# An attention and FFN kernel: transposed rows stored by GpSimd, transposes moved, and FFN seams interleaved with scores and V

## The reference

```python
# layer 1, for each of 8 batches; q = layernorm(x), k = v = cx
t = Wt @ v;  p = Wp @ q;  g = Wg @ k              # 512x512 by 512x2048
att = sum over each of 8 channel groups of p * g  # one number for a group
y = blockdiag(Wz) @ (att * t)                     # 8 blocks of 64x64
x = x + groupnorm(y) * gn_w + gn_b + v
# layer 2, for each row of layernorm(x), columns permuted, 16 heads of 128
h = gelu(t_head @ up[head])                       # 128 -> 512
out = h @ down[head]                              # 512 -> 128
x = x + unpermuted(out)
```

## Time and profile before

| | us |
|---|---|
| median of 3 runs | 1728.28 (1726.62 to 1729.94) |
| the profiled execution | 1731.32 |
| its span in the trace | 1729.5 |
| TensorE busy (matmuls) | 1550.4 (90%) |
| VectorE busy | 1306.9 (76%) |
| ScalarE busy | 919.1 (53%) |
| GpSimd busy | 718.4 (42%) |
| DMA, mean over the span | 218 GB/s |

### The profile page before, as it was taken

How to read it: one execution, slowest core, us unless ns; L and a number is a source line. 1 busy time by engine, 2 the same in 40 slices (tenths; PEclk the granted TensorE clock), 3 DMA queues, 4 the chain that set the end, 5 groups by cost and what they waited for, 6 DMA issues and landing times.

```text
span 1729.5 us, 19276 instructions
## 1 busy us (share of the span) xinstructions
PE 1550.4 (90%) x6592; PEld 1239.7 (72%) x6592; DVE 1306.9 (76%) x1872; ACT 919.1 (53%) x949; POOL 718.4 (42%) x589
## 2 busy tenths in 40 slices
PE   7898668789998899989999899998999889997998
PEld 6676556668776787767877677776877668765886
DVE  5767957877797868867698676987869786886665
ACT  4333425633576337843478234783357723676786
POOL 1333106301682117800287013960159301676785
PEclk9999989999999999999999999999999999999999
DMA  9988865785477835777266781769627693359675
GB/s 367 371 289 323 239 190 175 258 275 180 135 248 230 275 91 196 242 204 238 100 219 219 209 266 61 246 204 280 208 103 238 208 293 127 122 142 271 220 249 207
DMA packets 184512, 376.87 MB, mean 218 GB/s; under 512 B 24544, under 2 KB 98272, under 8 KB 176096
## 3 DMA queue, kind: packets, MB, share of 16 engines
q1 hardware_dynamic: 163936, 308.52, 55.5%
q0 software_dynamic: 20480, 67.13, 11.8%
HBM read 289.55 MB, written 86.03 MB: 217 GB/s over the span
## 4 chain that ended last, share of the span: by engine, by line
PE 42%; DVE 16%; DMA 9%; ACT 7%; issue 6%; SPq 4%; POOL 2%; POOLq 0%; DVEq 0%; ACTq 0%
PE PP L785 15%; PE PP L824 11%; PE PP L839 10%; PE PP L798 4%; DMA xg_scratch<-FB 4%; DVE Z L1051 3%; DMA RAW<-in_cT 3%; SPq L1249 3%; DVE FB L1083 3%; DVE R L1093 2%; PE PP L771 2%; ACT R L906 2%; DVE HX L1093 2%; DVE R L943 1%; DMA WW<-w_scratch 1%
## 5 line engine op out<-in xcount | busy, mean ns | idle before, releaser
L771 PE MATMUL PP<-R 128*128 128x512 f32 x1536 | 370.6, 398 | 65.4 <-DVE R L943 63.1
L824 PE MATMUL PP<-G,WW 128*128 128x512 f32 x1536 | 396.2, 395 | 17.9 <-DMA WW<-w_scratch 10.1
L785 PE MATMUL PP<-R,WC 128*128 128x512 f32 x1536 | 359.3, 396 | 37.1 <-ACT Z L876 28.5
L771 PEld LDWEIGHTS PP<-R 128*128 128x128 f32 x1536 | 289.0, 191 | 144.3 <-ACT R L864 44.5
L785 PEld LDWEIGHTS PP<-R,WC 128*128 128x128 f32 x1536 | 293.8, 192 | 101.8 <-ACT Z L876 30.3
L824 PEld LDWEIGHTS PP<-G,WW 128*128 128x128 f32 x1536 | 290.3, 191 | 88.6 <-issue 24.7
L839 PE MATMUL PP<-R,WW 128*128 128x512 f32 x1050 | 274.9, 398 | 43.8 <-DVE R L1093 32.7
L906 ACT ACTIVATE R<-PP 128x1024 fp32r<-128x1024 f32 x175 | 179.9, 1028 | 193.9 <-PE PP L824 193.0
L839 PEld LDWEIGHTS PP<-R,WW 128*128 128x128 f32 x1050 | 195.8, 190 | 96.3 <-issue 52.3
L907 ACT ACTIVATE PP<-PP 128x1024 f32<-128x1024 f32 x256 | 261.8, 1023 | 0.0
L864 ACT CAST R<-RAW 128x1024 fp32r<-128x1024 f32 x128 | 129.4, 1044 | 244.4 <-DMA RAW<-in_cT 225.7
(11 more groups left out here) (74 smaller groups left out, 1602.5 us busy)
## 6 DMA issues: line engine op xcount, KB each, us to landing
WW<-w_scratch SPq DMA_DIRECT2D x152, 512.0 KB, 5.2
RAW<-in_xT SPq DMA_DIRECT2D x64, 512.0 KB, 7.0
RAW<-in_cT SPq DMA_DIRECT2D x64, 512.0 KB, 8.1
X<-in_x SPq DMA_DIRECT2D x32, 1024.0 KB, 6.9
RAW<-in_cx SPq DMA_DIRECT2D x32, 1024.0 KB, 8.0
xg_scratch<-FB SPq DMA_DIRECT2D x112, 256.0 KB, 4.4
w_scratch<-WW SPq DMA_DIRECT2D x16, 1024.0 KB, 8.7
HX<-wp_scratch SPq DMA_DIRECT2D x8, 1024.0 KB, 9.1
```

What stands on the lines that cost most here:

```text
L771: t = eng.matmul(s_bank(c1), l[:, part(c1)], r, start=(dt == 0 and j == 0), stop=(dt == ND - 1 and j == 2))
L785: t = eng.matmul(PP[2 + ot // 2][:, ot % 2, :], WC[:, l, ct, part(ot)], u[:, r + ct, :], start=(ct == 0 and j == 0), stop=(ct == NT - 1 an ...
L824: t = eng.matmul(PP[slot["up", f, p]][:, e, :], wt[:, l, part(2 * p + e)], g[:, r, :], start=(j == 0), stop=(j == 2))
```

## The change

- `store_x` moves from SP to GpSimd, with the same wait for its block of transposes and the same four DMAs. The buffers and semaphores are the same.
- The four transpose blocks (and the stores, one step behind each) get due times from the table TURN, counted from the next batch's base: for batch 1 from 3.8, 6.8, 9.8, 12.8 to 4, 8, 12, 17.4; for batches 2 to 6 from 1.4, 4.4, 7.4, 10.4 to 3, 5.6, 9.6, 17.4. Batches 0 and 7 keep theirs.
- End of the FFN: `s_mm` becomes one stage for each column block. From batch 2 on the blocks of the first four steps are due by column: c1 = 0 of steps 0 to 3 from -1 to -0.4, then the last but one down step (0), c1 = 1 of the four steps (0.5 to 1.1), the last down step (1.5), and then c1 = 2 and 3. The splits of the first four steps move 1.8 steps ahead, those of steps 4 to 7 get times of their own (S_LATE), the first two loads move 2 steps ahead. The banks of up are counted from the end of the FFN, so that the last three use PP0, PP2, PP3 in this order and PP0 is free.
- Start of the FFN: the first up step goes to f0 - 1, ahead of V's last block (-0.5), the second to f0. `g_hi` and `g_lo` of the first unit move 0.7 ahead, `g_var_b` goes from f0 + 2.7 to f0 + 3.9, `x1_piece` from f0 + 4.8 to f0 + 5, `add_r` from td + 0.56 to td + 0.45.

```diff
--- before.py
+++ after.py
@@ -24,8 +24,12 @@
 EPS = 1e-5
 NRAW = 3
 NFB = 6
+TURN = [(17.9, 21.1, 24.3, 27.5), (4, 8, 12, 17.4)] + [(3, 5.6, 9.6, 17.4)] * 5
 SBT = 5
-UPS = (2, 3, 0)
+UPS = (0, 2, 3)
+S_EARLY = ([(-1 + 0.2 * dt, 0.5 + 0.2 * dt) for dt in range(4)],
+           [(2.0, 2.5), (2.25, 2.75), (3.0, 3.25), (3.5, 3.75)])
+S_LATE = {4: 2.55, 5: 2.8, 6: 3.3, 7: 4.4}
 
 
 def units(i):
@@ -121,14 +125,13 @@
         give(n.up("slo", i, dt), ("raw", slot["s", i, dt // 2]))
         order.append(("s_lo", i, dt))
 
-    def s_mm(i, dt):
+    def s_mm(i, dt, c1):
         if dt == 0:
-            for c1 in range(NT):
-                free["sb", i, c1] = take(("PP", c1 // 2, c1 % 2))
-        for c1 in range(NT):
-            t = n.up("smm", i, dt, c1)
-        give(t, s_half(i, dt))
-        order.append(("s_mm", i, dt))
+            free["sb", i, c1] = take(("PP", c1 // 2, c1 % 2))
+        t = n.up("smm", i, dt, c1)
+        if c1 == NT - 1:
+            give(t, s_half(i, dt))
+        order.append(("s_mm", i, dt, c1))
 
     def load_x(i, ct):
         free["x", i, ct] = take(("X", ct))
@@ -347,19 +350,16 @@
     def turn(i, q, ct):
         if ct == 0:
             if i < B - 1:
-                slot["tb", i, q] = None
-                free["tb", i, q] = take(*[("FB", k) for k in range(4)])
+                slot["tb", i, q] = [("FB", k) for k in range(4)]
             else:
-                k = slot["tb", i, q] = ring("raw", NRAW)
-                free["tb", i, q] = take(("raw", k))
+                slot["tb", i, q] = [("raw", ring("raw", NRAW))]
+            free["tb", i, q] = take(*slot["tb", i, q])
         t = n.up("tr", i, q, ct)
         give(t, ("Z", q, ct))
         order.append(("turn", i, q, ct))
 
     def store_x(i, q):
-        t = n.dma("xg", i, q, sem=f"xg{q}", count=4)
-        k = slot["tb", i, q]
-        give(t, *([("FB", k) for k in range(4)] if k is None else [("raw", k)]))
+        give(n.dma("xg", i, q, sem=f"xg{q}", count=4), *slot["tb", i, q])
         order.append(("store_x", i, q))
 
 
@@ -413,9 +413,9 @@
         give(n.up("radd", f), ("SM", b % 2))
         order.append(("resid", f, b))
 
-    def up_mm(f, p, kk, w):
-        slot["up", f, p] = UPS[kk % 3]
-        free["up", f, p] = take(*banks(UPS[kk % 3]))
+    def up_mm(f, p, k, w):
+        slot["up", f, p] = k
+        free["up", f, p] = take(*banks(k))
         t = n.up("up", f, p)
         give(t, ("WW", w % 2, 0))
         if p:
@@ -531,11 +531,13 @@
         y0, v0, f0 = s0 + 16, s0 + 32, s0 + 36
         first = i == 0
         for j in range(8):
-            put(s0 + 0.3 if (i, j) == (1, 2) else s0 + 2 * j - (5 if j or i else 10), load_s, i, j)
+            put(s0 + 0.3 if (i, j) == (1, 2) else s0 + 2 * j - (10 if i == j == 0 else 7 if i > 1 and j < 2 else 5), load_s, i, j)
         for dt in range(ND):
-            put(s0 + dt - 2.6, s_hi, i, dt)
-            put(s0 + dt - 2.4, s_lo, i, dt)
-            put(s0 + dt, s_mm, i, dt)
+            t = s0 + (dt - 2.6 if i < 2 else dt - 4.4 if dt < 4 else S_LATE.get(dt, dt - 2.6))
+            put(t, s_hi, i, dt)
+            put(t + 0.2, s_lo, i, dt)
+            for c1 in range(NT):
+                put(s0 + (dt + 0.25 * c1 if i < 2 or dt > 3 else S_EARLY[c1 // 2][dt][c1 % 2]), s_mm, i, dt, c1)
         for q in range(NQ):
             for ct in range(NT):
                 t = s0 + 8.4 + 2.6 * ct + 0.3 * q if i == 1 else s0 + (4 * q + ct) * 0.85 + (3.9 if first else 0.9)
@@ -573,21 +575,21 @@
         put(y0 + 1, load_wph, i)
         put(y0 + 12.1, load_wpl, i)
         for ot in range(NT):
-            put(v0 + ot, v_mm, i, ot)
-            put(v0 + ot + 0.95, v_att, i, ot)
+            put(v0 + ot + (0.5 if i and ot == NT - 1 else 0), v_mm, i, ot)
+            put(v0 + ot + (1.4 if i and ot == NT - 1 else 0.95), v_att, i, ot)
         put(v0 + 3.4, aggr_y, i)
         put(f0 + 1.2, g_mean_mm, i)
         put(f0 + 1.25, g_mean, i)
         put(f0 + 2.3, g_var_mm, i)
         put(f0 + 2.35, g_var_a, i)
         put(f0 + 2.4, g_root, i)
-        put(f0 + 2.7, g_var_b, i)
+        put(f0 + 3.9, g_var_b, i)
 
 
         last = i == B - 1
         sp = 2.6 if i < 2 else 4 if last else 6
         for ct in range(NT):
-            x0 = f0 + 4.8 + sp * ct
+            x0 = f0 + 5 + sp * ct
             for hf in range(2):
                 put(x0 + hf * sp / 6, x1_piece, i, ct, hf)
             for q in range(NQ):
@@ -603,7 +605,7 @@
         for ct in range(NT):
             put(e + 1 + 0.5 * ct if i == 0 else e + 1.6 + 0.8 * ct, xln2, i, ct)
         for q in range(NQ):
-            t = f0 + 17.9 + 3.2 * q if i == 0 else e + 4.6 + (2 if last else 3) * q
+            t = base[i + 1] + TURN[i][q] if not last else e + 4.6 + 2 * q
             for ct in range(NT):
                 put(t + 0.25 * ct, turn, i, q, ct)
             put(t + 1, store_x, i, q)
@@ -614,21 +616,23 @@
         end = len(gs)
         for g, (b, h, x) in enumerate(gs):
             lead = f0 + 2 * g
-            put(max(lead - 6, v0 - 2), gather, f, b, h)
-            put(lead - 2.3, g_hi, f, b)
-            put(lead - 2.1, g_lo, f, b)
+            put(max(lead - 6, v0 - 3 if g == 0 else v0 - 1), gather, f, b, h)
+            put(lead - (2.3 if g else 3.0), g_hi, f, b)
+            put(lead - (2.1 if g else 2.8), g_lo, f, b)
             put(lead - 1.5, resid, f, b)
             for p in range(2):
                 kk = 2 * g + p
-                tu = f0 + (kk - 1 if kk > 1 else 0.5 * kk)
-                td = f0 + (kk + 1.5 if kk < 2 * end - 2 else kk + 1 if kk < 2 * end - 1 else kk + 0.5)
-                td = min(td, f0 + 2 * end - (1 if kk == 2 * end - 2 else 0.5))
-                put(tu, up_mm, f, p, kk, w + x)
+                left = 2 * end - kk
+                tu = f0 + (kk - 1 if kk else -1)
+                td = f0 + kk + 1.5
+                if left < 3:
+                    td = f0 + 2 * end + (-0.5 * left if last else (1.5, 0)[left - 1])
+                put(tu, up_mm, f, p, UPS[(kk - 2 * end) % 3], w + x)
                 put(tu + 0.6, gelu, f, p, kk, i)
                 put(tu + 1.2, h_lo, f, p)
                 put(td, dn_mm, f, p, w + x)
                 w_used[w + x] = (tu + 0.55, td + 0.55)
-            put(min(td + 0.56, f0 + 2 * end - 0.01), add_r, f)
+            put(td + 0.45, add_r, f)
             put(td + 0.6, scatter, f, b, h)
             f += 1
         for x, (h, bs) in enumerate(ws):
@@ -738,8 +742,8 @@
         return PP[3][:, 1, :] if i == 0 else PP[1][:, 1, :]
 
     def tb_tile(i, q):
-        k = slot["tb", i, q]
-        t = FB[:, 0:4, :] if k is None else RAW[k][:]
+        name, k = slot["tb", i, q][0]
+        t = FB[:, 0:4, :] if name == "FB" else RAW[k][:]
         return t.rearrange("p a n -> p (a n)").rearrange("p (b c r) -> p b c r", b=16, c=4)
 
     def perm_of(h):
@@ -758,19 +762,18 @@
                     if ct % 2:
                         t.then_inc(S["wc"], 1)
             elif stage == "s_mm":
-                i, dt = a
+                i, dt, c1 = a
                 pe.wait_ge(*at["shi", i, dt])
                 pe.wait_ge(*at["slo", i, dt])
                 xh, ch = s_tile(i, dt, 0)[:, 0, :], s_tile(i, dt, 0)[:, 1, :]
                 xl, cl = s_tile(i, dt, 1)[:, 0, :], s_tile(i, dt, 1)[:, 1, :]
-                for c1 in range(NT):
-                    if dt == 0:
-                        for t in free["sb", i, c1]:
-                            pe.wait_ge(*t)
-                    for j, (l, r) in enumerate(((xl, ch), (xh, cl), (xh, ch))):
-                        t = eng.matmul(s_bank(c1), l[:, part(c1)], r, start=(dt == 0 and j == 0),
-                                       stop=(dt == ND - 1 and j == 2))
-                    t.then_inc(S["smm"], 1)
+                if dt == 0:
+                    for t in free["sb", i, c1]:
+                        pe.wait_ge(*t)
+                for j, (l, r) in enumerate(((xl, ch), (xh, cl), (xh, ch))):
+                    t = eng.matmul(s_bank(c1), l[:, part(c1)], r, start=(dt == 0 and j == 0),
+                                   stop=(dt == ND - 1 and j == 2))
+                t.then_inc(S["smm"], 1)
             elif stage == "y_mm":
                 i, q, ot = a
                 for t in free["y", i, q, ot]:
@@ -1148,6 +1151,13 @@
                 pool.wait_ge(*at["perm",])
                 eng.indirect_dma_start(out=FB[:, f % NFB, :], out_offset=None, in_=xg_d[b][:, :],
                                        in_offset=perm_of(h)).then_inc(S[f"fb{f % NFB}"], 16)
+            elif stage == "store_x":
+                i, q = a
+                pool.wait_ge(*at["tr", i, q, NT - 1])
+                for r in range(4):
+                    eng.dma_start(
+                        xg_d[i][cols(q), part(r)].rearrange("(b j) c -> j b c", j=32),
+                        tb_tile(i, q)[32 * r:32 * r + 32].rearrange("j b c r -> j b (c r)")).then_inc(S[f"xg{q}"], 16)
             elif stage == "resid":
                 f, b = a
```

(7 more changed lines are left out.)

## The result

| | before | after |
|---|---|---|
| median of runs in alternation (range), us | 1729.11 (1726.24 to 1735.05) | 1733.45 (1731.82 to 1736.72) |
| profiled execution, us | 1731.32 | 1731.82 |
| its span, us | 1729.5 | 1730.0 |

The ratio of the times is 1.0033, with a 95% interval of 1.0018 to 1.0048. The change makes the kernel 0.33% slower, 4 us by the medians and 6 by the ratio, where the prediction had 52 us faster. The time lies outside the range.

A forecast was written before the change was run, and what follows sets the result against it. TensorE was taken as the bound, its idle time as the price. Terms -24 (scores), -8 (batch 1's Y), -6 (FFN end), -18 (FFN start), +4 (last FFN) sum to -52 us: 1676 us from median 1728.28, range 1652 to 1722.

The forecast's parts named there:

- What bounds: Whole kernel: TensorE, busy 90% of the span, is the bound; a change is worth the TensorE idle time it removes.
- A block costs 5.6 us and lands 9.5 us after the transposes: Scores: GpSimd issues four stores at 1.4 us each; the block lands 3.9 us after its last issue, 3.5 steps after transposes.
- Block 0 ends at step 4, block 1 can then start at 7.5: Scores, batches 2 to 7: block 1, due at 5.6, costs 0.5 us; stage losses fall from 62 to 38, gain 24 us.
- The wait that I expected to cost 40 us or more: Sign to look for: the wait of VectorE's transposes for stores to land stays at 40 us or more.
- The fourth block in the Y stage: Last transpose block moved to step 17.4, in the next batch's Y stage; forecast difference there 0 us.
- Batch 1's Y stage: Without the store on SP the sums' broadcast goes out some 9 us earlier; gain 8 us, 15 us hole under 7.
- The end seam: FFN end into scores: early score blocks give the last down step 9.5 us; 1 of 3.4 us gained at six seams, 6 us.
- The start seam: FFN start: group variance behind the subtraction lets the fourth down step start earlier; 2.6 us at seven seams, 18 us gained.
- The last FFN stage: Sixteen stores at 1.4 us need 22.4 us of GpSimd's 14.5 us room; time lost, +4 us.
- (A): Rival: GpSimd's issue is slow, 2.5 us or more, and becomes the bound; total about 1762 us, slower; chance 14%.
- (B): Rival: DMA engines bound the scores, 48.8 us a stage; gain there only 12 us, total about 1698 us; chance 25%.
- (D): Rival: GpSimd as taken, but early score blocks wait so long for casts that all gains go; within 0.2%; chance 4%.

The follow-up runs named there:

- pool_only: Kernel before with only the store_x stores moved from SP to GpSimd, due times as before; 1769.65 us, ratio 1.0255.
- turn_only: Kernel before with only the transposes' new due times (3, 5.6, 9.6, 17.4), stores on SP; 1743.83 us, ratio 1.0103.
- after_oldturn: Changed kernel with transposes of batches 2 to 6 due at 3, 6, 9, 12 and batch 1's as before; 1772.74 us, ratio 1.0265.
- start_only: Kernel before with only the change's new order at the start of the FFN; 1707.82 us, ratio 0.9897.
- after_sp: Changed kernel with the stores put back on SP, all new due times kept; 1751.86 us, ratio 1.0135.

## Why the prediction was wrong

By its own steps:

- **What bounds** (TensorE, and its idle time is the price list): right, with one thing left out. A stretch of matmuls isn't always at 0.2267 us; the split above has to be made before a stage's loss is called idle time.
- **A block costs 5.6 us and lands 9.5 us after the transposes**: landing nearly right (9.9, 9.8 and 11.0 for blocks 0 to 2 by the semaphore, as the forecast counted), by two errors that cancel. The issue was 0.65 us, not 1.4, so the block is out in 2.6 to 3.1 us; and the landing is 7 to 8 us behind that, not 3.9, since the bytes share the DMA engines with the loads. The sentence "I add 0.5, since the bytes of the last two are still under way" took the whole of that.
- **"Block 0 ends at step 4, block 1 can then start at 7.5"**: this is the step that failed for the scores. It put a block's transposes at one step's length and on time. They take 5.4 us, spread among subtractions that wait for casts, so that block 0 ends at step 5.6 (batch 3), and the cycle is 15.6 us, not 12. Block 1 begins at step 9.4 and is then late by so much that the subtraction behind its first transpose leaves TensorE a hole (5.57 us in batch 3; 4.59, 4.72, 5.49 and 6.47 in 4 to 7; two of 2 us in batch 2). Forecast were 38 us of loss, measured 64.9.
- **The wait that I expected to cost 40 us or more** is 69.0 us. The relief of ScalarE (225.7 to 121.5) came in full, and the scores' loss didn't fall. In pool_only it came as well (116.6), beside 110.2 us of loss. So the wait for the loads, though the longest in the table, was not by itself what the scores lost.
- **The fourth block in the Y stage** was costed at nothing, with no cover named: 14 us. The runs tie it to the due time: all kernels with a block at 17.4 lose 12.7 to 26.2 us there (turn_only, with nothing else of the change, 22.0), and those without lose 0.5 to 4.1, after_oldturn among them (2.9), unless the small stores were moved into the stage. That the late gathers are what makes the sums' store land late is read from their rows and wasn't tested by itself.
- **Batch 1's Y stage**, -8: measured -6.7. Broadcast at 228.3 instead of 235.3, hole 6.56 us instead of 15.03, as predicted.
- **The end seam**, -6: measured +11 at five seams, and 14 to 21 in the time. The prediction gave the last down step its 9.5 us and looked only at the fourth score block's cast; it didn't ask what the moved casts and subtractions do to the down step before those. Of the +11, 2.6 are slow matmuls.
- **The start seam**, -18: measured -14 over batches 2 to 7, and start_only is 18 us faster than before. The fourth down step starts 1.36 us after its up step (659.48 and 658.12), as forecast. Batch 1 loses 2.6 us there instead of gaining.
- **The last FFN stage**, +4: measured -7.2, of it 3.1 in its start. 16 x 0.68 us of issues fit into the 14.5 us that the prediction had found, and SP's weight loads wait less: the hole of 7.63 us is now 3.44 at 1596.39.

**The rivals.** (A)'s slow issue isn't there, 0.65 us; the two-port rule of the Trainium skill, "SBUF — State Buffer", section "SBUF: two separate sides", isn't seen in these rows: 64 of the 112 issues ran beside a subtraction from two SBUF operands (L946) and took 0.651 to 0.741 us, and the longest of all took 0.911, so it was right to give it little. No row says which of VectorE's operations run in the two-port mode, so this speaks for these subtractions and not for the rule. One gather did take 2.68 us, at 401.84, beside a longer subtraction of the same kind, 2.28 us, begun at 401.41. (B) had the right place (the DMA engines) for the wrong reason: its sum went by their share, which fell to 0.81 in batch 6's scores where it was 0.91, and the loss lies in the latency of one block. Its sum also has a step without a row: 48.8 us a stage for 52.5 is 22 us over six stages, of which it took 12. (D), all gains going into waits, is the nearest, with 4%; it named only the early score blocks. No case had the transposes' landing take the place of the load.

The row of 12.25 us was held in the prediction against a rule of the Trainium skill, "DMA: Bandwidth & Descriptors", section "Issuing engines are not separate DMA queues": that another issuing engine saves the issue time only, since all share the 16 DMA engines. pool_only came out on the rule's side: ScalarE's wait for the loads did go (225.7 to 116.6), and it was 44 us slower. With the due times spread, the same move was worth 18 us (after_sp against the kernel after), so what a second issuing engine is worth was decided by who waits for the landing.

## What to carry to other kernels

Before a store is moved off a queue in which it holds loads back, ask what the loads will do to its landing, and who waits for the landing; where that is the next use of a single buffer, split the buffer first, which here was worth 27 us with the stores left on their queue. Price a moved block in the stage that receives it, by the one chain there that has a due time, and not by whether the stage has holes. And measure the parts of a change alone and each taken back: here -18, +18, +21 and +44 made +4. The stores and the due times, +44 and +18 alone, were each a gain beside the other; the FFN's start and end were worth in the change nearly what they were worth alone.

## What the runs showed of the hardware

- A plain store of 512 pieces of 512 bytes is issued by GpSimd in 0.65 us, four without a gap in 2.6 us. Its packets are of 4096 bytes (127168 packets in the kernel, 184512 before), where SP's are of 512; by block they took 0.16 to 0.29 us each on the mean, the small ones about 0.03.
- The last packet of the same 1 MB block ends 6.2 to 6.5 us after its transposes on SP's queue (7.8 with 1.5 MB beside it), 7.1 on GpSimd's with nothing beside it, and 9.3 to 10.5 with 1.4 to 1.8 MB of loads beside it.
- Eight stores of 4-byte pieces are followed by some 6 us in which the loads' 4096-byte packets take 0.91 us on the mean instead of 0.16; of those begun within 12 us of such a group, 31% took over 0.6 us, of the others 1.8%. Moving the group away, which also frees the queue, took 24 us off the scores' loss.
- After an idle stretch of 5.57 us TensorE's clock was at 0.50 for 4 us; with 22 matmuls by zeros in the stretch it was at 1.00. The scores' loss didn't fall with it.
